# Second attention: ScalarE takes the first head's exponential ahead of the projection's copy

## The reference, cut to what matters

```
q = decoder_output @ wq_w + wq_b          # layernorm(x), 112 rows a sequence
k = encoder_output @ wk_w + wk_b          # context, 375 rows a sequence
v = encoder_output @ wv_w + wv_b
score = einsum('bhqd,bhkd->bhqk', q, k) / sqrt(16)
score = score * mask
score = where(score == 0, -1e9, score)
alignment = softmax(score, axis=-1)
context = einsum('bhqk,bhkd->bhqd', alignment, v)
x = x + tanh(g_xattn[1]) * (context @ wo_w + wo_b)
```

## Time and profile before

| | |
|---|---|
| median of 3 runs | 1631.07 us (1628.36 to 1631.3) |
| profiled execution, its own time | 1624.04 us |
| its span | 1622.2 us |
| busy over the span | PE 1399.8, PEld 995.7, DVE 1230.6, ACT 1103.1, POOL 179.3 us |
| mean granted clock of TensorE | 0.936 |

### The profile page before, as it was taken

How to read it: one execution, slowest core, us unless ns; L and a number is a source line. 1 busy time by engine, 2 the same in 40 slices (tenths; PEclk the granted TensorE clock), 3 DMA queues, 4 the chain that set the end, 5 groups by cost and what they waited for, 6 DMA issues and landing times. The chain is left out here.

```text
span 1622.2 us, 40480 instructions
## 1 busy us (share of the span) xinstructions
PE 1399.8 (86%) x15436; PEld 995.7 (61%) x15436; DVE 1230.6 (76%) x3108; ACT 1103.1 (68%) x2440; POOL 179.3 (11%) x177
## 2 busy tenths in 40 slices
PE   5899999999999993492379898989898689999996
PEld 3577666666667662340366666666666367788884
DVE  5888888888888877758778999898898877344443
ACT  5777777777777763467428889888888654366663
POOL 1000001100000002200000000000000100034443
PEclk9999999999999997797688999999999889999998
DMA  6122232332322211000011121211010072122221
GB/s 206 46 86 85 85 107 90 96 107 85 98 93 91 76 60 59 0 1 26 0 57 50 54 77 54 77 51 28 18 35 12 21 251 68 56 35 46 49 45 23
DMA packets 64924, 105.67 MB, mean 65 GB/s; under 512 B 7449, under 2 KB 38914, under 8 KB 63586
## 3 DMA queue, kind: packets, MB, share of 16 engines
q1 hardware_dynamic: 58018, 94.83, 18.6%
q0 software_dynamic: 6720, 8.27, 3.2%
HBM read 68.88 MB, written 35.11 MB: 64 GB/s over the span
## 5 line engine op out<-in xcount | busy, mean ns | idle before, releaser
L1482 ACT ACTIVATE a_p<-a_s,a_nb 112x375 f32<-112x375 f32 x256 | 140.9, 598 | 26.5 <-DVE a_nb L1585 26.2
L271 PE MATMUL a_ps_o<-a_vh,a_pt 125*128 125x64 f16 (+1 forms) x1536 | 152.8, 183 | 2.6 <-ACT a_pt L1495 0.8
L1402 PE MATMUL a_ps_t<-ident,a_p 112*128 112x112 f32 x768 | 118.1, 284 | 42.6 <-ACT a_p L1482 41.3
L273 PE MATMUL a_ps_o<-a_vh,a_pt 125*128 125x64 f16 (+1 forms) x1536 | 151.1, 182 | 0.0
L272 PE MATMUL a_ps_o<-a_vl,a_pt 125*128 125x64 f16 (+1 forms) x1536 | 151.0, 182 | 0.0
L618 ACT ACTIVATE a_p<-a_ps_s,a_nb 112x375 f32<-112x375 f32 x256 | 144.0, 573 | 2.7 <-DVE a_scaled L768 2.1
L271 PEld LDWEIGHTS a_ps_o<-a_vh,a_pt 125*128 125x128 f16 x1536 | 133.5, 98 | 14.7 <-ACT a_pt L1495 6.4
L626 ACT ACTIVATE a_pt<-a_ps_t 125x336 f16<-125x336 f32 x256 | 101.5, 448 | 59.4 <-PE a_ps_t L555 59.1
L1402 PEld LDWEIGHTS a_ps_t<-ident,a_p 112*128 112x128 f32 x768 | 79.6, 146 | 97.8 <-issue 82.7
L272 PEld LDWEIGHTS a_ps_o<-a_vl,a_pt 125*128 125x128 f16 x1536 | 130.8, 98 | 11.0 <-issue 0.2
L1585 DVE CUSTOM_DVE_ANT_0 a_s<-a_s,a_fill 112x375 f32<-112x375 f32 x256 | 130.3, 547 | 5.5
(11 more groups left out here) (443 smaller groups left out, 4486.7 us busy)
## 6 DMA issues: line engine op xcount, KB each, us to landing
a_piece<-in_w SPq DMA_DIRECT2D x72, 256.0 KB, 3.0
split_weights<-a_pair SPq DMA_DIRECT2D x72, 256.0 KB, 3.3
w<-split_weights SPq DMA_DIRECT2D x8, 1024.0 KB, 6.1
a_ctx<-in_ctxT SPq DMA_DIRECT2D x16, 375.0 KB, 3.6
ctx<-a_cx SPq DMA_DIRECT2D x16, 375.0 KB, 4.2
a_cx<-ctx SPq DMA_DIRECT2D x16, 375.0 KB, 5.9
w1h<-split_weights SPq DMA_DIRECT2D x2, 1792.0 KB, 14.8
w1l<-split_weights SPq DMA_DIRECT2D x2, 1792.0 KB, 18.0
```

The source lines that it names most:

```text
L271: nc.tensor.matmul(out, wh, mh, start=(i == 0), stop=False)
L273: last = nc.tensor.matmul(out, wl, mh, start=False, stop=(i == n - 1))
L1402: mm = nc.tensor.matmul(ps_t[:, 2 * (g % 2) + i, t * S:(t + 1) * S], p32[:, g % 2, i, t * KV:t * KV + 128], ident32[0:S, 0:S], start=(t == ...
L1482: nc.scalar.activation(p32[:, g % 2, i, 0:NC], s2[:, g % 2, i, :], ACT.Exp, bias=nb[:, g % 2, i:i + 1], scale=-1.0).then_inc(exp_done, 1)
```

## The change

`exponentials` takes a list of heads. ScalarE's loop calls it for head 0 ahead of the job's copy and for head 1 behind it, where both exponentials stood behind the copy. No instruction is added or removed, and the streams of the other engines are the same; the line numbers behind the edit are two higher in the changed kernel.

```diff
-            def exponentials(g):
-                for i in range(2):
+            def exponentials(g, heads_of_pair):
+                for i in heads_of_pair:
                     act.wait_ge(max_ready, 2 * g + i + 1)
                     nc.scalar.activation(p32[:, g % 2, i, 0:NC], s2[:, g % 2, i, :], ACT.Exp,
                                          bias=nb[:, g % 2, i:i + 1], scale=-1.0).then_inc(exp_done, 1)
...
             for g in range(SLOTS):
                 if 0 <= g - 1 < G:
                     probabilities_high(g - 1)
+                if g < G:
+                    exponentials(g, (0,))
                 for name, b in slot_job(g):
                     if name != "W":
                         high(name, b)
                 if g < G:
-                    exponentials(g)
+                    exponentials(g, (1,))
                 if 0 <= g - 1 < G:
                     probabilities_low(g - 1)
```

## The result

The changed kernel takes 1714.89 us (median of 5 runs, 1701.36 to 1717.34), the kernel before 1628.36 beside it: a ratio of 1.0522, with a 95% interval of 1.0474 to 1.0571. Run again, it had 1.0545 (1.0524 to 1.0565). The forecast was 1711 us, +4.9%; it stood on the earlier median of 1631.07. The profiled execution was the fastest of the five (1701.36 us, span 1699.5); a second profile, of the repeated run, has a span of 1713.1, nearer to the median.

The account below looks back on a forecast made before the run. The prediction took a ring of waits among three nearly full engines as the bound. A closed VectorE-ScalarE ring (+67 us) and TensorE clock falls (+13) made +80 us, or 1711 us; the 8-in-10 range was 1690 to 1738.

Parts of the forecast that it names:

- A ring of waits: Second attention, 444 us: TensorE, VectorE and ScalarE each 85 to 89% full, none the bound alone.
- The ring's terms: Slots with a copy: masking to maximum 2.12, hand-overs, exponential 0.50, copy, low part; K and V 3.79 us, Q 5.30.
- The hand-over of 0.04: Semaphore between ScalarE and VectorE, taken as 0.04 us each way in a slot with a copy.
- A slot without a job: Slot with no copy, not in the ring: 2.70 us before and after, 15 of them making 40.5 us.
- The 15 W slots: Slots with the W job and no copy: 3.7 us each, bounds 2.89 and 4.7, 55.5 us together.
- The 0.4 us for a row of layernorm: 12 rows of layernorm standing in the ring, an estimated 0.4 us each, 4.8 us together.
- the clock's term: TensorE's clock falls behind the Q slot in 10 of 15 sequences at 1.35 us each: 13.5 us.
- the forecast's own 0.7 us: Time TensorE has left at full clock before the masking two slots on needs its work: some 0.7 us.
- The ring alone: Rival, chance 0.20: TensorE's clock stays as it was; +60 to +72 us, about 1698.
- The frequent lower clock: Rival, chance 0.15: a third of the 97 slots with a copy fall to the lower clock, 43 us more: 1741.
- Not slower: Rival, chance 0.03: the earlier exponential fills ScalarE's waits for the job's matmuls before K and V copies; 1609 us.
- no difference: Rival, chance 0.02: the copy is hidden anyway, so the sum is 0 and the time stays at 1631.

Follow-up runs that it names:

- the same useless copy inside and outside: Changed kernel plus one useless ScalarE copy per slot with a copy: between first exponential and job's copy 1746.43 us, at the slot's end 1714.80 us.
- the filled gap: Changed kernel plus 12 useless matmuls between the two heads' transposes of the Q slot's pair: 1708.09 us, ratio 1.0513 over the kernel before.
- the unsplit version: Kernel before, old order, with Q's high and low parts made by GpSimd: 1626.37 us, ratio 1.0007.
- the last version: Kernel before with Q's parts on GpSimd except the very first Q, and two of ScalarE's four Q copies behind the exponentials: 1613.83 us, ratio 0.9924.

## Why the prediction was right

**The bound.** "A ring of waits, and the busy table can't price a new order in it" held: busy times stayed and the phase grew by 78 us in the first profile. The pair with the same useless copy inside and outside shows it apart from the change: equal busy time, 31.6 us between them.

**The ring's terms.** The four kinds of slot, K, V, Q and K with a normalisation, were forecast at 3.79, 3.79, 5.30 and 4.41 us and measured at 3.78, 3.77, 5.28 and 4.40 wherever TensorE's clock did not lengthen them. The hand-over of 0.04, taken from one row, and the 0.50 of an exponential carried over unchanged.

**The slots outside the ring.** A slot without a job was taken at 2.70. Ten of the 15 came at 2.49 to 2.65, where VectorE has no gap (2.49 from one masking to the next, 1106.56 to 1109.05); the five of the last sequence took 4.00, 3.92, 2.59, 3.17 and 2.59, one of these with a normalisation. Without it all 15 took 41.1 us, and 47.2 in the second profile, against 40.5. The 15 W slots, taken at 3.7, took 3.70 and 3.81 on average without their layernorm rows; between short ones (2.89) and long ones (up to 4.7) that was the right middle. The 0.4 us for a row of layernorm was read from no row shown; it came at 0.32 (5.60 - 5.28 in the Q slots that have one).

**The sum.** 127 intervals were forecast at 500.4 for the ring and 513.9 with the clock's term, and took 511.1 and 525.6 in two profiles. By kind, with the layernorm rows and normalisations taken out:

| us | forecast | profile 1 | profile 2 |
|---|---|---|---|
| 82 slots with K, V, OT or X, clock's term included | 324.3 | 322.2 | 329.0 |
| 15 Q | 79.5 | 79.2 | 79.2 |
| 15 W | 55.5 | 55.6 | 57.1 |
| 15 without a job | 40.5 | 41.1 | 47.2 |

The time was +86.5 us by the medians beside each other and +90.5 in the repeat, against +80. The second profile, nearer to the median, shows where the difference lies: 7 us in the slots without a job and 5 in those with a copy.

**The clock's term had the right mechanism; its size came out by luck.** It was to come behind the Q slots in 10 of 15 sequences, at 1.35 us each. There the first V slot's clock was below full in 11 and 8 sequences of the two profiles, but all V slots together lost only 7.9 and 5.7 us by it. What I missed is the first K slot, behind the empty one: 5.02 to 5.52 us in seven sequences of the second profile, 11.4 us above its shortest in all. From sequence 1 on, the kernel before had nothing over 3.5 us there. Two such slots of the second profile, TensorE's windows over sequence 7's and sequence 8's (length, busy, clock, DMA share, GB/s), with DMA traffic in both and the clock down in one:

```profile
1080.17:1083.96 3.79, 3.51 (x42) 1.00 0.92 291
1111.96:1117.48 5.52, 5.35 (x39) 0.50 0.77 280
```

Over all 97 slots with a copy, 34 in the first profile and 43 in the second have a mean clock below full, and they cost 13.3 and 20.1 us above the ring's length, 0.4 to 0.5 us each; none at full clock is over 0.05 us above it. The forecast's 13.5 us is the first profile's number with three times fewer falls at three times the price. The price of 1.35 was read in an old slot that TensorE's lateness lengthened in full; in the ring TensorE has some time to spare (the forecast's own 0.7 us), so that much of a slow stretch is hidden; that is my reading of these averages and was not tested apart. The Trainium skill, "TensorE: Matmul & The Clock Gate", section "What's actually happening", which I had weighed, says that activity releases the throttle; the filled gap agrees, with one V slot below full clock where there were 17 and 12. But the two profiles of the changed kernel, with means of 0.84 and 0.78, have the same instructions, so the order of the work alone does not fix the mean.

**The rivals.** The ring alone (1698) was below all runs of the changed kernel, though the fastest, 1701.4, comes near. The frequent lower clock (1741; the range's top, explained in the same way, is 1738) was too much in time, but its condition came true: a third of the 97 slots, 32, was to fall, and 34 and 43 did. Its price was wrong, as above. Not slower and no difference are out by all runs. An unforeseen one, that the loss is the second exponential's lateness toward TensorE, was put up for the experiments and fell with both exponentials ahead of the copy.

## What to carry to other kernels

An instruction that waits for engine B, put ahead of one on engine A that B waits for, closes a ring between the two when B's next turn is queued behind that wait. Its length is the sum of both engines' steps plus the hand-overs; here it could be added up from rows of the old trace to 0.02 us, and no idle time on either engine shortened it. A third engine's slow stretches cost less on average inside this ring (0.4 to 0.5 us) than the one read before it (1.35), so an old price must be checked against the time that the ring leaves free. Put the work that the other engine waits for ahead of the work that waits for it. When the same busy time costs something at one place and nothing at another, the list to read is who stands behind the waiting instruction.

## What the runs showed of the hardware that was not expected

- GpSimd sat 7.08 us between its first cast and its first tensor-tensor subtraction on Q in this phase (7.47 us in the unsplit version), behind two MODIFY_POOL_CONFIG instructions of its sequencer that the trace lists right at the cast's end; in the later sequences it is 0.6 to 0.9 us from start to start. All engines waited for it there, and the first masking came 8.4 us later than before. The kernel before has the same pair at 832.0 us and the last version at 833.2, each ahead of 13 us in which GpSimd waits for VectorE, and lose nothing by it. That the pair is the gap's cause fits all four traces; no run moved it alone.
- The changed kernel's runs differ by 16 us (1701.36 to 1717.34), those of the kernel before by 9. In the two profiles of the changed kernel all ring-bound slots agree within 0.02 us; what differs is where TensorE's clock was low, mostly the first K slot of seven sequences and the slots without a job.
- ScalarE's copy of 376 columns from SBUF is listed with 0.50 us and takes 0.41 from its start to the next instruction's.
